# Interference stage of a complex-valued tower: inverse magnitudes moved from VectorE's reciprocal to ScalarE with a Newton step, four of the twelve weights begun on ScalarE, VectorE products joined

## The chip, the cores and the metric

The kernel is one program on one core of a Trainium2 chip. The metric is its device time in microseconds, the median of several executions. 0.2% (7 us) is about what a measurement can tell from no change.

## The reference, cut to what matters

A tower of 1024 tokens is encoded, passed through an attention, and then through the interference step below, with N = 4 complex vectors of D = 512 per token. R and I are the real and imaginary parts, `strength` is a 4x4 table per token (gathered embeddings).

```python
R = einsum('bnd,ned->bne', attn_r, int_Wr) - einsum('bnd,ned->bne', attn_i, int_Wi)
I = einsum('bnd,ned->bne', attn_r, int_Wi) + einsum('bnd,ned->bne', attn_i, int_Wr)
phase = arctan2(Ii * Rj - Ri * Ij, Ri * Rj + Ii * Ij)      # for every pair i, j
f = cos(phase) * strength[..., None]
sup_r = einsum('bijd,bjd->bd', f, R);  sup_i = einsum('bijd,bjd->bd', f, I)
norm = sqrt(sum(sup_r ** 2 + sup_i ** 2, axis=-1, keepdims=True) + 1e-08)
sup_r = sup_r / norm;  sup_i = sup_i / norm
```

The cosine of the phase between vectors i and j is the dot product of their unit vectors, element by element. The weight of vector j is strength[j,j] plus the sum over i of cosine(i,j) times strength[i,j].

## The kernel before

Five stages run one after the other: constants, first layers (tiles named a_), second layers (b_), attention (t_), interference (i_), top (e_). Only `phase_interfere` computes anything differently after the change. Its 1024 tokens are 8 tiles of 128. TensorE, for each tile and each n of 0 to 3, makes the real and the imaginary part of vector n, 48 matmuls of 128x512 in all (each product in three terms, L50 to L52), into one PSUM bank per part, so one tile fills all eight banks. Before it starts on vector n of tile t + 1, it waits for `unit`, that is, until VectorE has read vector n of tile t. It also waits for `negated`: ScalarE negates half of the loaded activations (`ng`, L1075), in a ring of two.

The tile then passes through three engines. `n` is the vector.

- ScalarE, `squares(t, n)`: square of the real part into `mag` (L1082) and of the imaginary part into `sqi` (L1085). The first may start only when the previous tile no longer needs `mag`.
- GpSimd, `add_squares`: their sum in `mag` (L1020).
- ScalarE, `magnitude(t, n)`: a mark for zero length (`zero`, Relu, L1089) and the root (`mag`, Sqrt, L1090).
- VectorE, `invert(n)`: reciprocal into `inv` (L1167). `unit_vector(n)`: both PSUM banks times `inv` into `cs` (L1175).
- The cosines of the pairs. Three of the six (`HELPED`: 0-1, 0-2, 1-2) are made by GpSimd, two products (L1037) and a sum (L1039) each; the other three by VectorE (L1188 to L1190). VectorE adds the mark `zz` (L1181, L1185 or L1191), and adds the cosine times its strength to two weights, which share the buffer of `inv`: L1199 where the weight is begun, L1196 afterwards.
- VectorE: weights times `mag` (L1223), then `cs` times weights for each part (L1225, two instructions of 2048 elements).
- GpSimd, `fold`: two sums over the four vectors (L1026, L1030). ScalarE and VectorE then scale `sup` by the inverse of its length (L1094 to L1100, L1152), a tile later.

GpSimd's order is fixed in its body: sums of squares 0 and 1, fold 0 of the last tile, sum of squares 2, fold 1, cosine 0-1, sum of squares 3, cosine 0-2, cosine 1-2. VectorE runs strictly in its program's order, and a `link` makes it wait for its own last instruction. Tiles 2 to 7 are turns of a hardware loop on VectorE and GpSimd. The top stage starts when the last `sup` is stored.

Of the kernel before, what the change touches and what calls it, by code (L numbers as in the profile page):

```python
# [9 lines left out]
ACT = mybir.ActivationFunctionType  # L10
# [4 lines left out]
P = 128  # L15
# [39 lines left out]
class Stage:  # L55


    def __init__(self, nc, tag):
        self.nc, self.tag, self.ctx = nc, tag, ExitStack()
# [4 lines left out]
    def sem(self, name):  # L64
        return self.ctx.enter_context(self.nc.semaphore(f"{self.tag}_{name}"))
# [5 lines left out]
def phase_constants(nc, g):  # L71
    s = Stage(nc, "c")
    with s.ctx:
        zeroed = s.sem("zeroed")
        made = s.sem("made")
        cols_in = s.sem("cols_in")
        block = s.ctx.enter_context(nc.Block())
# [29 lines left out]
def phase_first_layers(nc, g):  # L107
    s = Stage(nc, "a")
    XRAW = 4
    with s.ctx:  # L110
# [7 lines left out]
        hst = s.sb("hst", [P, TT, W])  # L118
        x_loaded = [s.sem(f"x_loaded{i}") for i in range(XRAW)]
        x_hi = s.sem("x_hi")  # L120
        x_split = s.sem("x_split")
        w_loaded = [s.sem(f"w_loaded{i}") for i in range(RAW)]
# [6 lines left out]
        bias_in = s.sem("bias_in")  # L129
        stored = [s.sem(f"stored{i}") for i in range(TT)]  # L130
# [105 lines left out]
def phase_second_layers(nc, g):  # L236
# [4 lines left out]
    with s.ctx:  # L241
# [42 lines left out]
        def _(pool):  # L284
# [4 lines left out]

            load_h(0, 0)  # L290
# [636 lines left out]
def phase_interfere(nc, g):  # L927
# [7 lines left out]
    STEPS = N + 1 + 3 * 2 + 3 * 4 + 1  # L935
    with s.ctx:
# [10 lines left out]
        t1 = s.sb("t1", [P, W])  # L947
        t2 = s.sb("t2", [P, W])
# [23 lines left out]
        chain = s.sem("chain")  # L972
        weighed = s.sem("weighed")
# [43 lines left out]
        def _(pool):  # L1017
# [4 lines left out]
            def fold(t, i):  # L1022

                if i == 0:
                    pool.wait_ge(weighed, t * 2 + 2)
# [44 lines left out]
        def _(act):  # L1070
# [7 lines left out]
            def squares(t, n):  # L1078
                act.wait_ge(multiplied, t * 8 + (2 * n + 2))
                if not (isinstance(t, int) and t == 0):  # L1080
                    act.wait_ge(chain, t * STEPS)
                act.activation(mag[:, n, :], g.ps[:, n, :], ACT.Square).then_inc(squared, 1)  # L1082
                if not isinstance(t, int) or 4 * t + n >= 2:
                    act.wait_ge(summed, t * N + (n - 1))
                act.activation(sqi[:, n % 2, :], g.ps[:, N + n, :], ACT.Square).then_inc(squared, 1)  # L1085

            def magnitude(t, n):
                act.wait_ge(summed, t * N + (n + 1))
# [3 lines left out]
            def length(t):  # L1092
                act.wait_ge(folded, t * 2 + 2)
                act.activation(sqi[:, :, :], sup[:, :, :], ACT.Square, accum_out=nrm[:, 0:1]).then_inc(len_done, 1)  # L1094
# [15 lines left out]
            def body(t, first, last=False):  # L1110
                squares(t, 0)
                if first:
                    negate(t, 2)
                magnitude(t, 0)
                squares(t, 1)
                if first:
                    negate(t, 3)
                magnitude(t, 1)
                squares(t, 2)
                magnitude(t, 2)  # L1120
# [17 lines left out]
            length(TT - 1)  # L1138
# [3 lines left out]
        def _(dve):  # L1142
# [5 lines left out]
            w = inv  # L1148
# [5 lines left out]
            def body(t, first):  # L1154
# [8 lines left out]
                def invert(n):  # L1163
                    dve.wait_ge(mag_done, t * N + (n + 1))
                    if not first and n == 0:
                        dve.wait_ge(weighed, t * 2)
                    link(dve.reciprocal(inv[:, n, :], mag[:, n, :]))  # L1167

                def unit_vector(n):
                    if not first and n == 0:  # L1170
                        dve.wait_ge(folded, (t - 1) * 2 + 1)
                    if not first and n == 2:
                        dve.wait_ge(folded, (t - 1) * 2 + 2)
                    for part in range(2):
                        dve.tensor_tensor(cs[:, part, n, :], g.ps[:, part * N + n, :], inv[:, n, :], ALU.mult).then_inc(unit, 1)  # L1175

                seen = set()

                def pair(i, j):

                    mark = dve.tensor_tensor(zz[:, :], zero[:, i, :], zero[:, j, :], ALU.add)  # L1181
                    if (i, j) in HELPED:
                        link(mark)
                        dve.wait_ge(helped, t * 9 + 3 * (HELPED.index((i, j)) + 1))
                        dve.tensor_tensor(t1[:, :], pc[:, 0, :], zz[:, :], ALU.add).then_inc(taken, 1)  # L1185
                        dve.wait_ge(taken, t * 3 + (HELPED.index((i, j)) + 1))
                    else:
                        dve.tensor_tensor(t1[:, :], cs[:, 0, i, :], cs[:, 0, j, :], ALU.mult)  # L1188
                        link(dve.tensor_tensor(t2[:, :], cs[:, 1, i, :], cs[:, 1, j, :], ALU.mult))
                        link(dve.tensor_tensor(t1[:, :], t1[:, :], t2[:, :], ALU.add))  # L1190
                        link(dve.tensor_tensor(t1[:, :], t1[:, :], zz[:, :], ALU.add))  # L1191
                    for a, b in ((i, j), (j, i)):

                        e = st[:, a * N + b:a * N + b + 1]
                        if b in seen:
                            ins = dve.scalar_tensor_tensor(out=w[:, b, :], in0=t1[:, :], scalar=e, in1=w[:, b, :],  # L1196
                                                           op0=ALU.mult, op1=ALU.add)
                        else:
                            ins = dve.tensor_scalar(w[:, b, :], t1[:, :], e, st[:, b * N + b:b * N + b + 1],  # L1199
                                                    ALU.mult, ALU.add)  # L1200
                            seen.add(b)
                    link(ins)

                invert(0)
                invert(1)
                unit_vector(0)
                unit_vector(1)
                invert(2)
                unit_vector(2)
                link(dve.tensor_copy(st[:, :], emb[:, bass.ds(t, 1), :].rearrange("p o x -> p (o x)")))  # L1210
                dve.wait_ge(unit, t * 8 + 12)
                pair(0, 1)
                invert(3)
                unit_vector(3)
                dve.wait_ge(unit, t * 8 + 16)
                pair(0, 2)
                pair(0, 3)
                pair(1, 2)
                if not first:
                    inverse_length(t - 1)  # L1220
                pair(1, 3)
                pair(2, 3)
# [513 lines left out]
```

## Time and profile before

| | us |
|---|---|
| median of 3 runs | 3566.72 (3565.09 to 3569.43) |
| span of the profiled execution | 3548.6 |
| interference stage in it, from its first weight load to the store of the last `sup` | 2807.3 to 3296.8 |
| last final multiplication ends | 3286.9 |

The profiled span starts at the first instruction and ends at the last; the 18.1 us between it and the median lie around it. In a row, the number behind the engine is the line of the kernel, and what stands in square brackets is how long the engine was idle before the instruction and what ended that. A group's row gives the shortest, the median and the longest duration in ns.

### The profile page before, as it was taken

The numbers are of one execution on the slowest core, as the hardware profiler recorded it, in microseconds if no ns is written. First come the engines' busy times: TensorE is split into PE (matmuls) and PEld (weight loads), VectorE is DVE, ScalarE is ACT, GpSimd is POOL, SyncE is SP. The second block draws the span as 40 slices with busy tenths as digits, with TensorE's granted clock in tenths as the row PEclk, the third lists the DMA queues.
The fourth block names the chain that finished last, engine by engine and source line by source line (L and its number), as shares of the span: only waits on it lengthen the run. The fifth ranks groups of instructions, "written<-read, shape, count | busy, mean of one in ns | idle before, by whom it ended". The sixth has DMA issues, their size and how long they took to land. (4 is left out here: it accounts for less than half of the span.)

```text
span 3548.6 us, 45531 instructions
## 1 busy us (share of the span) xinstructions
PE 3115.3 (88%) x16160; PEld 2659.5 (75%) x16160; DVE 1652.0 (47%) x3027; ACT 1168.9 (33%) x1986; POOL 388.2 (11%) x345
## 2 busy tenths in 40 slices
PE   8999999996999899995889989898989598884586
PEld 6888888885888788874778878887878476763575
DVE  3222222226211341114665566556655579999322
ACT  3111111114211241114554555455555432332332
POOL 1000000001111110010000000000000244543100
PEclk9999999998999999997998989898989799997798
DMA  5222222214333333323212221122112553442210
GB/s 181 71 71 71 71 71 71 71 59 163 113 95 95 113 118 94 93 74 128 78 47 56 62 71 47 49 70 71 47 47 72 136 102 83 89 85 45 95 36 6
DMA packets 364201, 285.38 MB, mean 80 GB/s; under 512 B 280048, under 2 KB 280176, under 8 KB 364016
## 3 DMA queue, kind: packets, MB, share of 16 engines
q1 hardware_dynamic: 341488, 206.97, 21.6%
q0 software_dynamic: 22656, 77.67, 6.3%
q8 instruction: 33, 0.54, 0.1%
q14 instruction: 24, 0.20, 0.0%
HBM read 194.40 MB, written 90.18 MB: 80 GB/s over the span
## 5 line engine op out<-in xcount | busy, mean ns | idle before, releaser
L50 PE MATMUL banks<-a_whi,a_xhi 128*128 128x512 f32 x1152 | 449.9, 391 | 24.0 <-DVE a_wlo L175 17.6
L51 PE MATMUL banks<-a_wlo,a_xhi 128*128 128x512 f32 x1152 | 448.8, 390 | 0.0
L52 PE MATMUL banks<-a_whi,a_xlo 128*128 128x512 f32 x1152 | 448.8, 390 | 0.0
L50 PE MATMUL banks<-b_ghi,b_whi 128*128 128x512 f32 x1024 | 401.8, 392 | 9.9 <-DVE b_slo L383 8.6
L51 PE MATMUL banks<-b_glo,b_whi 128*128 128x512 f32 x1024 | 398.9, 390 | 0.0
L52 PE MATMUL banks<-b_ghi,b_wlo 128*128 128x512 f32 x1024 | 398.8, 389 | 0.0
L175 DVE TENSOR_TENSOR a_wlo<-a_wraw,a_whi 128x512 fp32r<-128x512 f32 x144 | 99.6, 692 | 577.2 <-ACT a_whi L161 577.2
L50 PE MATMUL banks<-t_sx,t_whi 128*128 128x256 f32 x1024 | 307.7, 300 | 36.8 <-DVE t_wlo L791 26.9
L161 ACT ACTIVATE a_whi<-a_wraw 128x512 fp32r<-128x512 f32 x144 | 90.9, 632 | 667.7 <-PE banks L52 628.9
L51 PE MATMUL banks<-t_sx,t_whi 128*128 128x256 f32 x1024 | 295.7, 289 | 0.0
L368 DVE TENSOR_TENSOR b_wlo<-b_wraw,b_whi 128x512 fp32r<-128x512 f32 x128 | 88.2, 690 | 444.8 <-ACT b_whi L320 444.6
L52 PE MATMUL banks<-t_sx,t_wlo 128*128 128x256 f32 x1024 | 294.5, 288 | 0.0
L708 DVE TENSOR_SCALAR t_ks<-banks,cols 64x256 f32<-64x256 f32 x512 | 247.4, 483 | 97.5 <-PE banks L52 86.4
L50 PEld LDWEIGHTS banks<-a_whi,a_xhi 128*128 128x128 f32 x1152 | 216.6, 188 | 72.0 <-issue 17.6
L52 PEld LDWEIGHTS banks<-a_whi,a_xlo 128*128 128x128 f32 x1152 | 216.6, 188 | 45.2
L51 PEld LDWEIGHTS banks<-a_wlo,a_xhi 128*128 128x128 f32 x1152 | 216.7, 188 | 44.8
L50 PEld LDWEIGHTS banks<-t_sx,t_whi 128*128 128x128 f32 x1024 | 203.5, 199 | 43.2 <-DVE t_wlo L791 27.5
L50 PEld LDWEIGHTS banks<-b_ghi,b_whi 128*128 128x128 f32 x1024 | 192.7, 188 | 54.9 <-DVE b_slo L383 13.1
L320 ACT ACTIVATE b_whi<-b_wraw 128x512 fp32r<-128x512 f32 x128 | 80.2, 628 | 458.2 <-PE banks L52 457.5
L50 PE MATMUL banks<-i_whi,i_ax 128*128 128x512 f32 x384 | 159.3, 415 | 72.6 <-ACT i_ng L1075 38.1
L52 PEld LDWEIGHTS banks<-b_ghi,b_wlo 128*128 128x128 f32 x1024 | 192.4, 188 | 40.1
L51 PEld LDWEIGHTS banks<-b_glo,b_whi 128*128 128x128 f32 x1024 | 192.7, 188 | 39.0
(192 smaller groups left out, 6208.8 us busy)
## 6 DMA issues: line engine op xcount, KB each, us to landing
a_wraw<-w_first SPq DMA_DIRECT2D x144, 256.0 KB, 2.6
b_wraw<-w_second SPq DMA_DIRECT2D x128, 256.0 KB, 2.7
t_sx<-s_scr SPq DMA_DIRECT2D x64, 512.0 KB, 5.5
a_scr<-t_at SPq DMA_DIRECT2D x256, 128.0 KB, 1.9
i_ax<-a_scr SPq DMA_DIRECT2D x64, 512.0 KB, 5.9
h_scr<-a_hst POOLq DMA_DIRECT2D x72, 256.0 KB, 2.7
b_hl<-h_scr POOLq DMA_DIRECT2D x16, 1024.0 KB, 6.0
s_scr<-b_shi POOLq DMA_DIRECT2D x32, 512.0 KB, 4.4
```

The costliest lines, as they stand in the source:

```text
L50: mm(out, ahi, bhi, start=first, stop=False)
L51: mm(out, ahi, blo, start=False, stop=False)
L52: return mm(out, alo, bhi, start=False, stop=last)
L161: act.activation(whi[:, k % SPL, :], wraw[:, k % RAW, :], ACT.Copy).then_inc(w_hi, 1)
L175: dve.tensor_tensor(wlo[:, k % SPL, :], wraw[:, k % RAW, :], whi[:, k % SPL, :].bitcast(F32), ALU.subtract).then_inc(w_split, 1)
L320: act.activation(whi[:, j % SPL, :, :].rearrange("p a n -> p (a n)"), wraw[:, j % RAW, :], ACT.Copy).then_inc(w_hi, 1)
L368: dve.tensor_tensor(wlo[:, j % SPL, :, :].rearrange("p a n -> p (a n)"), wraw[:, j % RAW, :], whi[:, j % SPL, :, :].bitcast(F32).rearrange ...
L708: ins = dve.tensor_scalar(ks[half(at_half), m % 2, h, part, :], b_qk[half(h), 1, e * C:(e + 1) * C], bcol(M_K + e, m, half(h)), float(sign ...
```

## The change

Per tile, in the interference stage:

- VectorE's four reciprocals of 512 go. For two vectors at a time (q is 0 or 1), ScalarE takes the root s = Abs_reciprocal_sqrt(mag) and squares it, so y = s*s is roughly 1/mag. VectorE then does a Newton step, `tt = mag*y` and `inv = (tt - 2)*y` (that is minus 1/mag; the sign is undone in `rescale`).
- Relu, Sqrt and the two new activations run on 1024 elements. They wait for the sums of both vectors.
- The unit vectors of two n are one multiplication of 2048 elements out of four PSUM banks, which are renumbered by `bank(n, part)`. TensorE waits for two vectors at once.
- VectorE's own cosines take one product of 1024 in place of two of 512. The order of pairs becomes 0-1, 0-3, 0-2, 1-3, 1-2, 2-3.
- The copy of the strengths and the four instructions that begin the weights move to ScalarE (`strengths`, `begin`). GpSimd's second and third cosine wait for these.
- The multiplication by `mag` becomes two `rescale` of 1024, the first of which releases `mag` for vectors 0 and 1 before pair 2-3. The final multiplication is one of 4096.
- `negate` stands elsewhere in ScalarE's order, the scaling of `sup` comes after the begun weights.
- Outside the stage, GpSimd clears 11 semaphores at the start of the second layers, and semaphores are allocated in another order.

```diff
+    def bank(n, part):
+        return 4 * (n // 2) + 2 * part + n % 2
@@ gpsimd
-                pool.wait_ge(unit, t * 8 + (2 * N + 2 * j + 2))
-                pool.wait_ge(taken, t * 3 + x)
+                pool.wait_ge(unit, t * 2 + (j // 2 + 1 + 2))
+                if x == 0: ...
+                elif x == 1:
+                    pool.wait_ge(w_begun, t * 4 + 2)
+                else:
+                    pool.wait_ge(w_begun, t * 4 + 4)
+                    pool.wait_ge(taken, t * 3 + 1)
@@ scalar
+            def magnitude(t, q):
+                n = slice(2 * q, 2 * q + 2)
+                act.wait_ge(summed, t * N + (2 * q + 2))
+                act.activation(zero[:, n, :], mag[:, n, :], ACT.Relu, scale=-1.0 / LEAST, bias=k01[:, 1:2])
+                act.activation(mag[:, n, :], mag[:, n, :], ACT.Sqrt, bias=k01[:, 0:1]).then_inc(mag_done, 1)
+                act.wait_ge(mag_done, t * 6 + (3 * q + 1))
+                act.activation(sqi[:, :, :], mag[:, n, :], ACT.Abs_reciprocal_sqrt).then_inc(mag_done, 1)
+                act.wait_ge(mag_done, t * 6 + (3 * q + 2))
+                act.activation(sqi[:, :, :], sqi[:, :, :], ACT.Square).then_inc(mag_done, 1)
...
             def body(t, first, last=False):
+                negate(t, 3)
                 squares(t, 0)
-                if first:
-                    negate(t, 2)
+                squares(t, 1)
                 magnitude(t, 0)
-                squares(t, 1)
-                magnitude(t, 1)
                 squares(t, 2)
-                magnitude(t, 2)
                 if not last:
                     negate(t + 1, 0)
                 squares(t, 3)
-                magnitude(t, 3)
+                magnitude(t, 1)
+                strengths(t)
+                begin(t, 0, 1, 0, pc[:, 0, :], True)
                 if not last:
                     negate(t + 1, 1)
                 if not first:
-                    length(t - 1)
-                    scale(t - 1)
+                    length(t - 1, t * STEPS + SEED_READ[1])
+                begin(t, 0, 3, 1, tt[:, 0, :])
+                begin(t, 0, 2, 2, pc[:, 0, :])
                 if not last:
                     negate(t + 1, 2)
-                    negate(t + 1, 3)
+                if not first:
+                    scale(t - 1)
@@ vector
+                def unit_vectors(q):
+                    n = slice(2 * q, 2 * q + 2)
+                    dve.wait_ge(mag_done, t * 6 + (3 * q + 3))
+                    link(dve.tensor_tensor(tt[:, :, :], mag[:, n, :], sqi[:, :, :], ALU.mult))
+                    if not first:
+                        dve.wait_ge(weighed, t)
+                    link(dve.scalar_tensor_tensor(out=inv[:, n, :], in0=tt[:, :, :], scalar=2.0, in1=sqi[:, :, :],
+                                                  op0=ALU.subtract, op1=ALU.mult))
+                    if not first:
+                        dve.wait_ge(folded, t * 2 - (1 - q))
+                    dve.tensor_tensor(cs[:, :, n, :], g.ps[:, 4 * q:4 * q + 4, :]..., inv[:, n, :]..., ALU.mult).then_inc(unit, 1)
...
+                unit_vectors(0)
+                cosine(0, 1)
+                unit_vectors(1)
+                p = cosine(0, 3)
+                dve.wait_ge(w_begun, t * 4 + 2)
+                weigh(p, 3, 0)
+                p = cosine(0, 2)
+                weigh(p, 2, 0, taken)
+                dve.wait_ge(w_begun, t * 4 + 3)
+                p = cosine(1, 3)
+                weigh(p, 1, 3)
+                weigh(p, 3, 1)
+                dve.wait_ge(w_begun, t * 4 + 4)
+                p = cosine(1, 2)
+                weigh(p, 1, 2, taken)
+                weigh(p, 2, 1, taken)
+                dve.wait_ge(taken, t * 3 + 3)
+                rescale(0)
                 if not first:
                     inverse_length(t - 1)
+                p = cosine(2, 3)
+                weigh(p, 2, 3)
+                weigh(p, 3, 2)
+                rescale(1)
+                dve.wait_ge(w_scaled, t * 2 + 2)
+                dve.tensor_tensor(cs[:, :, :, :], cs[:, :, :, :], inv[:, :, :]..., ALU.mult).then_inc(weighed, 1)
```

`squares(t, n)` now waits for `rescale` of its pair in the tile before, and its second square, into `sqi`, for the Newton step that reads `sqi` last.

## Rows read from the trace of the kernel before

**Rows 1.** Busy time in a stretch of the stage: columns as in the first line.
```profile
core 0: us, PE busy (x) PEld busy (x) DVE busy (x) ACT busy (x) POOL busy (x), PEclk, DMA share, GB/s
2900.00:3000.00 100.00, 88.47 (x376) 70.70 (x374) 97.33 (x90) 30.23 (x53) 50.94 (x30) 0.98 0.43 88
```

**Rows 2.** Timeline of GpSimd: the first sum of squares of two tiles.
```profile
2959.86 2.28 POOL L1020 TENSOR_TENSOR i_mag<-i_mag,i_sqi 128x512 f32<-128x512 f32 x1 [19.20 <-ACT i_sqi L1085]
...
3013.89 2.27 POOL L1020 TENSOR_TENSOR i_mag<-i_mag,i_sqi 128x512 f32<-128x512 f32 x1 [19.63 <-ACT i_sqi L1085]
```

**Rows 3.** Timeline of TensorE: the first matmul of a third vector (n = 2).
```profile
3003.74 0.77 PE L50 MATMUL banks<-i_whi,i_ax 128*128 128x512 f32 x1 [6.00 <-ACT i_ng L1075]
```

**Rows 4.** Groups on the weights' and inverses' tile: ns min/median/max, first and last start.
```profile
L1196 DVE SCALAR_TENSOR_TENSOR i_inv<-i_t,i_st,i_inv x64: 743/750/1780, 2883.9 to 3279.3; 128x512 f32<-128x512 f32 x64
L1167 DVE RECIPROCAL i_inv<-i_mag x32: 3342/3353/3355, 2854.8 to 3253.6; 128x512 f32<-128x512 f32 x32
L1199 DVE TENSOR_SCALAR i_inv<-i_t,i_st x32: 540/1518/1621, 2871.9 to 3266.9; 128x512 f32<-128x512 f32 x32
...
L1223 DVE TENSOR_TENSOR i_inv<-i_inv,i_mag x8: 2291/2292/2294, 2903.9 to 3280.1; 128x2048 f32<-128x2048 f32 x8
```

**Rows 5.** Groups on the unit vectors' tile.
```profile
L1175 DVE TENSOR_TENSOR i_cs<-banks,i_inv x64: 679/681/693, 2861.9 to 3257.6; 128x512 f32<-128x512 f32 x64
...
L1026 POOL TENSOR_TENSOR i_cs<-i_cs x8: 4492/4612/4623, 2913.3 to 3287.0; 128x2048 f32<-128x2048 f32 x8
L1030 POOL TENSOR_TENSOR i_sup<-i_cs x8: 2337/2416/2437, 2919.2 to 3291.5; 128x1024 f32<-128x1024 f32 x8
```

**Rows 6.** Group on the magnitudes' tile.
```profile
L1020 POOL TENSOR_TENSOR i_mag<-i_mag,i_sqi x32: 1267/1294/2282, 2850.6 to 3247.7; 128x512 f32<-128x512 f32 x32
```

**Rows 7.** ScalarE, groups of the stage: busy us, mean ns | idle before.
```profile
L1100 ACT ACTIVATE i_sup<-i_sup,i_nrm 128x1024 f32<-128x1024 f32 x8 | 9.2, 1148 | 121.6 <-DVE i_nrm L1152 121.6
L1094 ACT ACTIVATE i_sqi<-i_sup 128x1024 f32<-128x1024 f32 x8 | 8.4, 1046 | 21.7 <-POOL i_sup L1030 21.7
```

**Rows 8.** Timeline of VectorE and GpSimd around cosine 1-2 of the third tile.
```profile
2988.52 0.43 DVE L1181 TENSOR_TENSOR i_zz<-i_zero 128x512 bf16<-128x512 bf16 x1
2989.07 0.69 DVE L1185 TENSOR_TENSOR i_t<-i_pc,i_zz 128x512 f32<-128x512 f32 x1
2989.80 1.62 DVE L1199 TENSOR_SCALAR i_inv<-i_t,i_st 128x512 f32<-128x512 f32 x1
2989.84 2.73 POOL L1037 TENSOR_TENSOR i_pc<-i_cs 128x512 f32<-128x512 f32 x2 [5.00 <-DVE i_t L1185]
2991.34 1.78 DVE L1196 SCALAR_TENSOR_TENSOR i_inv<-i_t,i_st,i_inv 128x512 f32<-128x512 f32 x1
2992.64 1.62 POOL L1039 TENSOR_TENSOR i_pc<-i_pc 128x512 f32<-128x512 f32 x1
2993.15 1.40 DVE L1181 TENSOR_TENSOR i_zz<-i_zero 128x512 bf16<-128x512 bf16 x1
```

**Rows 9.** Timeline where a tile begins: what runs beside fold 0.
```profile
2964.32 6.83 DVE L1167 RECIPROCAL i_inv<-i_mag 128x512 f32<-128x512 f32 x2
...
2965.80 4.62 POOL L1026 TENSOR_TENSOR i_cs<-i_cs 128x2048 f32<-128x2048 f32 x1
```

**Rows 10.** ScalarE's table loads: the interference stage's one, and a group of the attention.
```profile
2852.66 1.28 ACT L1090 ACT_TABLE_LOAD   x1
...
L671 ACT ACT_TABLE_LOAD x64 | 82.1, 1283 | 1.1
```

**Rows 11.** Timelines: the first tile's last squares, its final and the last final multiplications.
```profile
2873.65 0.60 ACT L1082 ACTIVATE i_mag<-banks 128x512 f32<-128x512 f32 x1 [3.75 <-PE banks L52]
...
2906.26 5.57 DVE L1225 TENSOR_TENSOR i_cs<-i_cs,i_inv 128x2048 f32<-128x2048 f32 x2
...
3282.40 4.49 DVE L1225 TENSOR_TENSOR i_cs<-i_cs,i_inv 128x2048 f32<-128x2048 f32 x2
```

**Rows 12.** GpSimd: the shortest instruction of the stage.
```profile
L1054 POOL MEMSET i_k<- 128x1 f32 x1 | 0.1, 98 | 1206.7 <-POOLq L500 1206.7
```

More of the change, by code:

```diff
@@ L1080, in squares @@
                 if not (isinstance(t, int) and t == 0):
[L1081 to L1088, printed above, removed]
+                    act.wait_ge(w_scaled, t * 2 - (1 - n // 2))
@@ new lines, in squares @@
+                act.activation(mag[:, n, :], g.ps[:, bank(n, 0), :], ACT.Square).then_inc(squared, 1)
+                if n >= 2:
+                    act.wait_ge(chain, t * STEPS + SEED_READ[0])
+                elif not (isinstance(t, int) and t == 0):
+                    act.wait_ge(chain, t * STEPS - (STEPS - SEED_READ[1]))
+                act.activation(sqi[:, n % 2, :], g.ps[:, bank(n, 1), :], ACT.Square).then_inc(squared, 1)
+            def magnitude(t, q):
+                n = slice(2 * q, 2 * q + 2)
+                act.wait_ge(summed, t * N + (2 * q + 2))
@@ new lines, in strengths, with begin @@
+            def strengths(t):
+                if not (isinstance(t, int) and t == 0):
+                    act.wait_ge(w_scaled, t * 2)
+                act.activation(st[:, :], emb[:, bass.ds(t, 1), :].rearrange("p o x -> p (o x)"), ACT.Copy).then_inc(st_in, 1)
+            def begin(t, i, j, order, of, both=False):
+                act.wait_ge(st_in, t + 1)
+                act.wait_ge(p_made, t * 3 + (order + 1))
+                for a, b in ((i, j), (j, i)) if both else ((i, j),):
+                    ins = act.activation(inv[:, b, :], of, ACT.Identity, scale=st[:, a * N + b:a * N + b + 1],
+                                         bias=st[:, b * N + b:b * N + b + 1])
+                    ins.then_inc(w_begun, 1)
@@ L1161, in link @@
                     dve.wait_ge(chain, t * STEPS + done[0])
[L1163 to L1175, printed above, removed]
@@ L1177, in body @@
[L1177 to L1181 removed]
+                def unit_vectors(q):
[8 more added lines that the diff above has]
+                        dve.wait_ge(folded, t * 2 - (1 - q))
+                    dve.tensor_tensor(cs[:, :, n, :], g.ps[:, 4 * q:4 * q + 4, :].rearrange("p (a n) w -> p a n w", a=2),
+                                      inv[:, n, :].unsqueeze(1).to_broadcast([P, 2, 2, W]), ALU.mult).then_inc(unit, 1)
+                    dve.wait_ge(unit, t * 2 + (q + 1 + 2))
@@ new lines, in cosine, with weigh, rescale @@
+                    return p
+                def weigh(p, a, b, last=None):
+                    ins = dve.scalar_tensor_tensor(out=inv[:, b, :], in0=p, scalar=st[:, a * N + b:a * N + b + 1],
+                                                   in1=inv[:, b, :], op0=ALU.mult, op1=ALU.add)
+                    if last is None:
+                        link(ins)
+                    else:
+                        ins.then_inc(last, 1)
+                def rescale(q):
+                    n = slice(2 * q, 2 * q + 2)
+                    dve.scalar_tensor_tensor(out=inv[:, n, :], in0=inv[:, n, :], scalar=-1.0, in1=mag[:, n, :],
+                                             op0=ALU.mult, op1=ALU.mult).then_inc(w_scaled, 1)
@@ L1219, in body @@
+                weigh(p, 1, 2, taken)
+                weigh(p, 2, 1, taken)
+                dve.wait_ge(taken, t * 3 + 3)
+                rescale(0)
                 if not first:
                     inverse_length(t - 1)
-                pair(1, 3)
-                pair(2, 3)
-                link(dve.tensor_tensor(w[:, :, :], w[:, :, :], mag[:, :, :], ALU.mult))
-                for part in range(2):
-                    dve.tensor_tensor(cs[:, part, :, :], cs[:, part, :, :], w[:, :, :], ALU.mult).then_inc(weighed, 1)
+                p = cosine(2, 3)
```

92 lines of the change are left out of this document (43 added, 49 removed).

## Prediction

> **What bounds the kernel now.** I looked first at where the changed stage lies in the span, then at how busy each engine is in it, then at one tile in the timelines. In the stage VectorE is busy 97% of the time, TensorE 88%, GpSimd 51% and ScalarE 30% [rows 1]. A tile takes 54.0 us: GpSimd's first sum of squares starts at 2959.86 in one and at 3013.89 in the next [rows 2]. TensorE's share of that is 0.87 x 54.0, some 47 us, and where it pauses it waits for `ng` [rows 3], which ScalarE makes late because it stands behind the scaling of `sup`, which waits for VectorE. So TensorE has some 7 us of slack per tile, and VectorE in its program's order sets the period. The obvious cost is the reciprocal, four of 3.35 us per tile [rows 4].
>
> Less obvious is what shares VectorE's time. Its instructions have two durations: the update of a weight 0.75 us or 1.78, the beginning of one 0.54 or 1.5 to 1.6 [rows 4]. The timeline shows which [rows 8]. GpSimd starts two products at 2989.84; VectorE's L1199 ends 1.07 us late, L1196 1.03 late, and the mark (0.43 when alone) 0.97 late. GpSimd's sum in its turn takes 1.62 in place of 1.29, and its sums of squares reach 2.28 [rows 6]. They take turns, an instruction each: one runs, the other waits for it to end. That holds for VectorE's instructions that read two tiles of SBUF and for L1199. It does not hold for the reciprocal, of which two take 6.83 us beside GpSimd's fold [rows 9], nor for the multiplication out of PSUM, of which the longest of 64 is 0.693 [rows 5]. In the kernel before, these two kinds fill exactly the time in which GpSimd folds (4.61 and 2.42 us [rows 5]) and sums.
>
> **The change, part by part.** Prices first. Two inputs of 512 take 0.69 us and of 2048 take 2.29 [rows 4, 8], so 1.04 ns per element more: 1.23 for 1024, 4.43 for 4096. The Newton step and `rescale`, of L1196's kind, take 0.75 + 0.53 = 1.28. The joined multiplication out of PSUM takes 0.68 + 1.60 = 2.28 [rows 5]. A wait for the own last instruction adds 0.04 [rows 8]. ScalarE's 1024 elements take 1.15 with a pointer for scale or bias (Relu, Sqrt) and 1.05 without (root, square) [rows 7]; I take 0.09 off where the next one does not wait.
>
> On VectorE itself this saves: 13.4 of reciprocals for 4 x 1.28 or so (5.1), four begun weights (2.2 alone, some 5 as they ran), and about 1.5 in the joined instructions. That is some 12 us per tile of work, and it would be the gain if VectorE stayed busy. I do not think it does. So I lay out one tile of the loop in order, with 0 at the end of the final multiplication of the tile before.
>
> 1. Fold 0 starts at once on GpSimd, 4.6 us. VectorE is next at `tt = mag*sqi`, which reads two SBUF tiles, so it is held until 4.65. (The turn of VectorE's loop is hidden below this.) Before, two reciprocals ran here.
> 2. `tt` 1.27, Newton 1.32, both unit vectors 2.28: 9.5.
> 3. GpSimd's next in order is the sum of squares 2. ScalarE can only write its `sqi` after the Newton step has read it (7.2), plus 0.6 for the square: the sum runs from 7.9 to 9.1, fold 1 to 11.5. VectorE's mark for pair 0-1 waits behind fold 1: 2.0 us.
> 4. GpSimd makes cosine 0-1, three instructions, 11.8 to 15.65. VectorE has nothing else in its order. The sum of squares 3 stands right behind on GpSimd and holds VectorE's join until 16.9.
> 5. Now ScalarE can begin on vectors 2 and 3: Relu, Sqrt, root, square, 4.3 with their waits, plus the table loads. The trace shows 1.28 for a load [rows 10]. It does not show whether Sqrt and Abs_reciprocal_sqrt share a table. The bounds are none and one at each change. The nearest rows are those of the attention, whose group has a load in each of its 64 steps where two functions alternate, so I take one before Sqrt and one before the root, 2.6 us: square done at 23.8. VectorE is idle from 17.6.
> 6. Unit vectors of 2 and 3, 4.9: 28.7.
> 7. Pair 0-3: mark, product of 1024, two sums, one weight, 4.0. GpSimd's cosine 0-2 runs beside it, three turns of 1.25 less the 0.13 gap, 3.4: 36.1. Pair 0-2: 2.0. Pair 1-3 with two weights 4.8, and cosine 1-2 beside it 3.4. Pair 1-2: 2.8. That is 49.1.
> 8. `rescale(0)` 1.2 and the small reciprocal 0.1: 50.4. It releases `mag`, so the next tile's squares and their two sums fall on pair 2-3 and the second `rescale`: 4.8 + 1.3 + 2 x 1.12 = 8.3. Final multiplication 4.4: 63.0.
>
> So the period is 63.0 against 54.0. The next tile's first magnitudes are ready in time: squares at 51.5, sums by 56, four activations and a load 5.6, some 62, before the fold is over. TensorE is released for vectors 0 and 1 at 9.5 and does them in 23.5. For the third it waits for `negate`, which stands behind the last begun weight (38.2) and is done at 39.4; for the fourth again, since that `negate` stands behind the scaling of `sup` (51.5) and is done at 52.7. Its last matmul ends at 64, or 66 with the slow start after a pause (0.77 us for a matmul [rows 3]). ScalarE asks for it at 63 + 8, behind the other squares, so some 5 us of cover are left; a load that came later than that would lengthen the tile. GpSimd's added waits (`w_begun`) end before VectorE's own pair does. The strengths' copy and the four begun weights lie on ScalarE, in idle time.
>
> The trace does not show a fold of 4.6 us against an instruction of two inputs, only sums of 1.29. Its bounds are 4.6 of holding, or, if the two share, none; I take 4.6, since every pair of rows 8 waits to the end. Without it the Newton step is done at 2.6 and the sum of squares 2 follows fold 0 directly, so item 3 ends 3.2 earlier.
>
> The first tile: its last squares start at 2873.65 [rows 11]. Add 1.1 for them, 1.3 for the sum, 6.9 for item 5, 4.9 for item 6 and 34.3 for items 7 and 8: 2922.1, against 2906.26 + 5.57 = 2911.8 before, 10.3 later. Seven tiles follow, 7 x 63.0, the last without a next tile's sums (2.3): 438.7, end 3360.8, against 3282.40 + 4.49 = 3286.9 before: 73.9 later. The last length needs a table load, 1.3. The 11 clears on GpSimd stand before its first load of the second layers; each is at least nothing and at most like its shortest instruction, 0.10 [rows 12], so 0 to 1.1, and I take 0.5. Sum: +75.7. The profiled span would be 3548.6 + 75.7 = 3624, and the median, 18.1 above it as before, **3642 us**, 2.1% slower.
>
> Two rules of the Trainium skill bear on this. "SBUF — State Buffer", section Who interferes with whom, has VectorE with two SBUF inputs and a GpSimd instruction that reads SBUF exclude each other for the whole instruction. Rows 8 agree for 1.29 us (1.03 late); by the rule the fold holds `tt` for its whole 4.6, which no row here shows. "ScalarE: Activation LUTs", section What ACT_TABLE_LOAD costs, counts a load as 1.28 and a drain of 1.38. The trace has the 1.28, and Sqrt began 0.02 after it, with no drain, so I leave the drain out. By the page a tile would take some 65.6 us and the kernel 3663. Its section Table sets has one expensive function per set, which would make these loads certain.
>
> **The rivals.**
>
> - *No loads, or a fold that does not hold.* One table serves both functions: 2.6 less per tile in eight, and 1.3 at the end, +54, 3621. With the fold free as well, 3.2 x 7 less: 3599.
> - *The turns are not taken where instructions are joined, and it gets faster* (the other side). For it: the product out of PSUM and the reciprocal never wait. Against it: rows 8, where three different kinds of instruction with SBUF inputs wait. Without any turns GpSimd reaches the end of its sum 3 at 13.3 in place of 16.9 (fold 0 at 4.65, the sum 1.25, fold 1 2.4, the cosine 3.8, the sum 1.25), item 7 loses 6.8 and item 8 loses 2.2: 12.6 less, 50.4 per tile. The first tile then ends 1.3 later than before, seven tiles take 352.8 against 375.1, and 1.8 is for the last load and the clears: -19, 3547. With no loads either, 48.0 per tile and 3527. The sum moves by 94.9 for these 12.6, so it decides at 10.1 less per tile, a period of 52.9.
> - *The change does all that it says*: VectorE, GpSimd and ScalarE hide behind TensorE. Then seven tiles take 47 in place of 375.1 / 7 = 53.6, 46 less, 3521. Against it is the order of GpSimd's body: cosine 0-1 is behind two folds, and magnitudes 2 and 3 behind that.
> - *TensorE becomes the bound at its lower clock.* It would pause some 16 us per tile in place of some 6 [rows 3]. If it stayed at the slow spacing (0.43 for 0.23) a tile would take 48 x 4 x 0.43 = 82 us and the kernel some 3790. Against it: with one pause per tile the granted clock of the stretch is still 0.98, nearly the full 2.4 GHz [rows 1].
>
> **How the numbers follow.** Forecast (61 to 66 per tile, 3628 to 3668): 0.72. No loads or a weaker fold (3597 to 3628): 0.11. Slow TensorE: 0.04. The turns not taken, or all hidden: 0.10. Within 0.2%: 0.03. The range 3597 to 3668 takes the first two, 0.83. Its upper end allows 1.5 per tile for the turn of the loop, if it is not hidden (a tile outside the loop took 2964.3 - 2911.8 = 52.5 [rows 9, 11], one in it 54.0), one more load of 1.28 per tile on the path, and 4 in the rest. Slower is 0.72 + 0.11 + 0.04 = 0.87, same 0.03, faster 0.10.
>
> **What the profile after would show.** ScalarE with some 4 table loads per tile, in magnitude and in length. VectorE's `tt` for vectors 0 and 1 with a longest of 4 to 5 us where 1.2 is its own, and ends with fold 0. VectorE idle before the join of pair 0-1 (GpSimd's cosine) and before `tt` of vectors 2 and 3 (ScalarE's square), together 8 to 10 us per tile. VectorE below 85% busy, TensorE near 75%, with its pause now ended by the unit vectors. A tile of 60 to 66 us from final multiplication to final multiplication. I am wrong if `tt` runs at 1.2 beside the fold, if the loads are missing, or if VectorE is busy throughout.

## Result: 3642.9 us against 3566.0, 2.2% slower

The changed kernel takes 3642.94 us (median of 4 executions, 3603.05 to 3649.15), the kernel before 3566.01 (4 executions, 3565.09 to 3569.43) on the same chip. The ratio is 1.0219, 95% interval 1.0143 to 1.0296. The forecast was 3642. A second set of 6 executions gave 3643.66 and 1.0228 (1.0166 to 1.029). Two executions of the runs below, 3765.63 us of sum3_early and 4194.97 of begin_alone, had a much lower clock than the others of their kernel and are in no ratio.

### The profile page after: what moved, and what is told of

Read it like the earlier page. It is cut to its first block and busy times, and to the rows that moved or that the text cites. A ratio compares the mean times of both kernels' runs of the same rounds, so it can differ in the third digit from the quotient of the medians.

```text
span 3647.3 us, 45563 instructions
## 1 busy us (share of the span) xinstructions
PE 3133.1 (86%) x16160; PEld 2673.5 (73%) x16160; DVE 1599.1 (44%) x2915; ACT 1277.3 (35%) x2069; POOL 426.4 (12%) x345
## 5 line engine op out<-in xcount | busy, mean ns | idle before, releaser
L50 PE MATMUL banks<-t_sx,t_whi 128*128 128x256 f32 x1024 | 308.3, 301 | 36.9 <-DVE t_wlo L797 27.5
```

The costliest lines, as they stand in the source:

```text
L50: mm(out, ahi, bhi, start=first, stop=False)
```

## The profile after

First the stretch view, as in [rows 1]. I give it for one tile, from one fold 0 to the next. The first fence is the kernel before, the second the changed kernel.

```profile
2965.80:3019.82 54.02, 46.16 (x193) 36.81 (x192) 52.25 (x51) 16.32 (x28) 25.23 (x17) 0.94 0.41 86
```

```profile
3003.78:3068.09 64.31, 48.20 (x193) 38.21 (x193) 43.85 (x36) 30.55 (x39) 31.47 (x17) 0.89 0.35 74
```

VectorE (the third busy time) went from 52.25 us per tile to 43.85: the change took 8.4 us of work off it, as it says. The tile grew by 10.3 us all the same. VectorE is now busy 68% of it, TensorE 75%, and no engine is the bound by its work. What bounds is the order in which the engines hand over. The view of waits, of the changed kernel from 2900 to 3300, names the hand-overs (total us, times, longest us):

```profile
DVE i_tt L1207 <- ACT i_sqi L1118: 87.6, 12, 8.3
...
ACT i_zero L1113 <- POOL i_mag L1034: 78.5, 12, 7.0
...
PE banks L50 <- DVE i_cs L1214: 53.4, 6, 10.1
...
DVE i_pc L1228 <- POOL i_pc L1060: 22.7, 6, 3.8
```

VectorE waits for ScalarE's square (L1118) twice per tile, ScalarE waits for GpSimd's sums, and VectorE waits for GpSimd's cosine 0-1. Now one tile's beginning in the timeline of the changed kernel, the place that answers to [rows 2, 8, 9] (rows of the three engines by start):

```profile
2991.40 1.15 ACT L1142 ACTIVATE i_sup<-i_sup,i_nrm 128x1024 f32<-128x1024 f32 x1 [10.45 <-DVE i_nrm L1193]
2992.57 1.28 ACT L1096 ACT_TABLE_LOAD   x1
2993.86 1.15 ACT L1096 ACTIVATE i_ng<-i_ax 128x512 fp32r<-128x512 f32 x2
2994.92 0.58 ACT L1103 ACTIVATE i_mag<-banks 128x512 f32<-128x512 f32 x1
...
2996.01 1.22 DVE L1246 SCALAR_TENSOR_TENSOR i_inv<-i_inv,i_mag 128x1024 f32<-128x1024 f32 x1
2996.06 7.76 POOL L1034 TENSOR_TENSOR i_mag<-i_mag,i_sqi 128x512 f32<-128x512 f32 x2 [10.79 <-ACT i_sqi L1108]
2997.27 5.40 DVE L1274 TENSOR_TENSOR i_cs<-i_cs,i_inv 128x4096 f32<-128x4096 f32 x1
3003.78 4.55 POOL L1040 TENSOR_TENSOR i_cs<-i_cs 128x2048 f32<-128x2048 f32 x1
3003.85 1.15 ACT L1113 ACTIVATE i_zero<-i_mag,i_k 128x1024 bf16<-128x1024 f32 x1 [6.89 <-POOL i_mag L1034]
3005.01 1.28 ACT L1114 ACT_TABLE_LOAD   x1
3006.30 1.15 ACT L1114 ACTIVATE i_mag<-i_mag,i_k 128x1024 f32<-128x1024 f32 x1
3007.47 1.28 ACT L1116 ACT_TABLE_LOAD   x1
3008.76 1.06 ACT L1116 ACTIVATE i_sqi<-i_mag 128x1024 f32<-128x1024 f32 x1
3009.85 1.06 ACT L1118 ACTIVATE i_sqi<-i_sqi 128x1024 f32<-128x1024 f32 x1
3010.94 1.23 DVE L1207 TENSOR_TENSOR i_tt<-i_mag,i_sqi 128x1024 f32<-128x1024 f32 x1 [8.27 <-ACT i_sqi L1118]
...
3021.79 1.76 DVE L1228 TENSOR_TENSOR i_pc<-i_pc,i_zz 128x512 f32<-128x512 f32 x1 [3.78 <-POOL i_pc L1060]
...
3030.14 1.22 DVE L1207 TENSOR_TENSOR i_tt<-i_mag,i_sqi 128x1024 f32<-128x1024 f32 x1 [6.58 <-ACT i_sqi L1118]
```

Read it from the GpSimd row at 2996.06. Two sums of squares, 1.27 us each when nothing stands in their way, take 7.76: the first runs when `rescale(1)` (L1246) is done, the second only when the final multiplication of 4096 elements (L1274) is done at 3002.67. That multiplication itself takes 5.40 in place of 4.43, since the first sum goes before it. Relu for the next tile starts at 3003.85, beside fold 0, with two table loads behind it, and VectorE's `tt` is 8.27 us late. ScalarE reached these squares late because it does the scaling of `sup`, a table load and a negation first (2991.40 to 2994.9). At 3021.79 VectorE waits 3.78 for cosine 0-1, at 3030.14 6.58 for the square of vectors 2 and 3. The three waits together are 18.6 us per tile.

Two groups give the turn-taking in durations (ns min/median/max), and four the table loads (us busy, mean ns), from 2870 to 3395:

```profile
L1207 DVE TENSOR_TENSOR i_tt<-i_mag,i_sqi x16: 1218/1226/5495, 2888.0 to 3348.5; 128x1024 f32<-128x1024 f32 x16
L1034 POOL TENSOR_TENSOR i_mag<-i_mag,i_sqi x32: 1262/1292/5476, 2878.2 to 3340.2; 128x512 f32<-128x512 f32 x32
```

```profile
L1116 ACT ACT_TABLE_LOAD x16 | 20.5, 1283 | 0.3
L1114 ACT ACT_TABLE_LOAD x15 | 19.2, 1283 | 0.1
L1138 ACT ACT_TABLE_LOAD x7 | 9.0, 1283 | 0.1
L1096 ACT ACT_TABLE_LOAD x6 | 7.7, 1283 | 7.8 <-DMA i_ax<-a_scr 7.7
```

There are 44 loads, six in a tile of the loop. Last, the ends of the first and last final multiplication, which answer to [rows 11]:

```profile
2938.44 4.43 DVE L1274 TENSOR_TENSOR i_cs<-i_cs,i_inv 128x4096 f32<-128x4096 f32 x1
...
3379.89 4.43 DVE L1274 TENSOR_TENSOR i_cs<-i_cs,i_inv 128x4096 f32<-128x4096 f32 x1
```

3384.3 - 2942.9 = 441.4 for seven tiles; it was 375.1.

## The experiments

My theory: the longer chain (squares, sums, Relu, two loads, root, square, Newton step) lies on the tile's path, and whole-instruction turns between VectorE and GpSimd stretch it. The rivals were that something outside the stage's arithmetic costs the time, that the table loads cost all of it, or that the joined instructions or the begun weights do.

Every kernel was timed against the kernel before on its own chip. Executions of one kernel spread over as much as 50 us (last section), so I also give the period of a loop tile, fold 0 to fold 0, and the length of the stage from its profile, from the first load of the strengths' ids to the first load of the top stage. Before, these are 54.0 and 511.4; changed, 64.3 and 589.7, in a pair of profiles on one chip.

| | ratio (95%) | tile | stage |
|---|---|---|---|
| changed, again | 1.0228 (1.0166 to 1.029) | 64.3 | 589.7 |
| frame_only | 0.9983 (0.9956 to 1.001) | 54.0 | 511.1 |
| no_table_loads | 1.0103 (1.0053 to 1.0153) | 58.3 | 551.1 |
| sum3_early | 1.0131 (1.0083 to 1.0178) | 58.9 | 547.6 |
| reciprocal_back | 1.012 (1.0075 to 1.0164) | 58.6 | 556.3 |
| final_in_two | 1.019 (1.0107 to 1.0272) | 62.2 | 579.9 |
| three_repairs | 1.0036 (0.9993 to 1.0078) | 55.5 | 528.2 |
| begin_alone | 0.9917 (0.9875 to 0.9959) | 50.0 | 484.3 |
| joined_alone | 1.0049 (1.0008 to 1.009) | 55.6 to 55.9 | 523.2 |
| two_helped_begin | 0.9876 (0.9816 to 0.9937) | 48.4 | 474.0 |

The tiles came out where they were expected, but for reciprocal_back (58.6 for 60 to 62) and two_helped_begin (48.4, just under 48.5 to 51). Four medians fell below their expected ranges: reciprocal_back 3597.08 (3613 to 3628), begin_alone 3529.92 (3533 to 3550), two_helped_begin 3512.37 (3520 to 3540) and three_repairs 3567.85 (3570 to 3590).

**The changed program around the old stage.** The clears and the order of semaphores as after, `phase_interfere` as before.

> The stage of before inside the changed frame: the 11 clears on GpSimd and the new order of semaphores alone. Forecast's term: +0 to +1.1 us, same as before within 0.2%. Rival: the frame moves the start of the interference stage (it began 2.4 us later in the changed kernel, and TensorE then stood for 18.6 us between its first two vectors with nothing recorded); then this kernel is 2 to 20 us slower than before. If the 18.6 us pause is an accident of an execution and not of the change, it turns up in some profiles of either kernel.

Tile 54.0, stage 511.1, 3562.55 us: no difference. The clears cost nothing that shows, and the time is lost in the stage.

**No table loads.** The root becomes a function that is loaded already.

```diff
-act.activation(sqi[:, :, :], mag[:, n, :], ACT.Abs_reciprocal_sqrt)
+act.activation(sqi[:, :, :], mag[:, n, :], ACT.Sqrt)
```

> The changed kernel with Sqrt in the place of Abs_reciprocal_sqrt (the inverse magnitudes are then wrong numbers), so that ScalarE needs one table only; six loads of 1.28 us per tile go. Theory of the path (a tile is a line of hand-overs, and two loads lie on it in magnitude 1, and where the second sum of squares is held by the final multiplication two or three more): 58 to 62 us per tile in place of 64.3, 15 to 45 us less than the changed kernel, 3600 to 3628. Rival (the tile is as long as VectorE's own work with its turns, ScalarE is 35% busy and its loads are hidden): 64.3 per tile, no difference to the changed kernel.

The tile fell from 64.3 to 58.3: 6.0 us for six loads of 1.28 (7.7), so most of this time lies on the path, and still 4.3 of the 10.3 remain without any. Here the next tile's sums get in before the final multiplication, and the fold then does what item 1 of the forecast said. The timeline of this kernel:

```profile
3054.63 1.22 DVE L1207 TENSOR_TENSOR i_tt<-i_mag,i_sqi 128x1024 f32<-128x1024 f32 x1
...
3054.79 5.41 POOL L1040 TENSOR_TENSOR i_cs<-i_cs 128x2048 f32<-128x2048 f32 x1 [5.63 <-DVE i_cs L1274]
...
3055.88 5.40 DVE L1210 SCALAR_TENSOR_TENSOR i_inv<-i_tt,i_sqi 128x1024 f32<-128x1024 f32 x1
```

The fold waits for `tt` (5.41 in place of 4.6), then `inv = (tt - 2)*y` waits for the whole fold and takes 5.40 in place of 1.22. That is the price which no row of before showed: a fold holds an instruction of two SBUF inputs for all its length. The Trainium skill, "SBUF — State Buffer", section Who interferes with whom, states it so, and these rows agree with it at 4.6 us.

**The sum of squares 3 ahead of fold 1** on GpSimd.

```diff
                 add_squares(t, 2)
+                add_squares(t, 3)
                 if not first:
                     fold(t - 1, 1)
                 cosine(t, 0)
-                add_squares(t, 3)
```

> The changed kernel with GpSimd's sum of squares 3 in front of fold 1 and cosine 0-1; the same instructions. Theory of the path: ScalarE starts magnitude 1 some 7 us earlier, of which the later pair 0-1 gives back 1 to 2; 57 to 60 us per tile, 30 to 50 us less than the changed kernel, 3593 to 3613. Rival (VectorE's work and turns set the tile): as many instructions and turns as before, less than 1 us per tile, 3636 to 3649.

58.9, as expected: 5.4 us for moving a 1.27 us instruction past a fold and a cosine. ScalarE no longer waits for fold 1 and cosine 0-1 before it can go on with vectors 2 and 3. The price is in one row, where VectorE now waits longer for cosine 0-1:

```profile
3099.13 0.69 DVE L1228 TENSOR_TENSOR i_pc<-i_pc,i_zz 128x512 f32<-128x512 f32 x1 [7.38 <-POOL i_pc L1060]
```

**Reciprocal back**, joined (1024 elements), in place of root, square and Newton step; all else as changed.

```diff
-                    link(dve.tensor_tensor(tt[:, :, :], mag[:, n, :], sqi[:, :, :], ALU.mult))
...
-                    link(dve.scalar_tensor_tensor(out=inv[:, n, :], in0=tt[:, :, :], scalar=2.0, in1=sqi[:, :, :],
-                                                  op0=ALU.subtract, op1=ALU.mult))
+                    link(dve.reciprocal(inv[:, n, :], mag[:, n, :]))
```

> The changed kernel with the Newton step undone: VectorE's reciprocal on 1024 elements (6.7 us) for each pair of vectors, no root of a reciprocal, no square, no table loads; everything else as changed. Theory of the path: the first reciprocal runs beside the fold, which held VectorE anyway, the second takes 6.7 where load, load, root and square (4.7) and the two Newton instructions (2.6) were: 60 to 62 us per tile, 15 to 30 us less than the changed kernel, 3613 to 3628, though VectorE works 8 us more per tile. Rival (the Newton step saves its 8 us, and other parts of the change cost): 72 us per tile, 3700.

58.6, better than the 60 to 62 expected. The costliest instruction of the old profile comes back and the tile gets 5.7 us shorter. Two things could explain it: the table loads go with the root, and the reciprocal takes no turns. The timeline shows the second:

```profile
3077.89 4.53 POOL L1040 TENSOR_TENSOR i_cs<-i_cs 128x2048 f32<-128x2048 f32 x1 [5.62 <-DVE i_cs L1265]
...
3077.91 6.55 DVE L1202 RECIPROCAL i_inv<-i_mag 128x1024 f32<-128x1024 f32 x1
```

The reciprocal's 6.55 us cover the fold's 4.53 completely, neither is stretched. But no_table_loads keeps the Newton step, drops only the loads, and has 58.3. So the 5.7 us are what the loads cost. The choice between reciprocal and Newton step, without loads, is worth 0.2 us, although the Newton step takes 8.2 us less of VectorE per tile (four of 1.22 for two of 6.55). Where those go can be read from the two timelines, each counted from the end of the final multiplication:

- Unit vectors 0 and 1 are done at 9.1 in both. The 4.1 us that VectorE saves there are the 4.2 by which the fold holds it.
- Cosine 0-1 is joined 1.7 later with the Newton step (16.7 for 15.0), because the square of vector 2 must wait until that step has read `sqi`, and GpSimd stands still for it (1.79). In reciprocal_back it waits for GpSimd's earlier sum alone.
- For vectors 2 and 3 the root and the square on ScalarE add 2.2 before VectorE can start. Of the second 4.1 saved, 1.9 is left.

The row is of no_table_loads, where VectorE starts on vectors 2 and 3:

```profile
3075.33 1.23 DVE L1207 TENSOR_TENSOR i_tt<-i_mag,i_sqi 128x1024 f32<-128x1024 f32 x1 [3.90 <-ACT i_sqi L1118]
```

**The final multiplication in two of 2048.**

```diff
-                dve.tensor_tensor(cs[:, :, :, :], cs[:, :, :, :], inv..., ALU.mult).then_inc(weighed, 1)
+                dve.tensor_tensor(cs[:, 0, :, :], cs[:, 0, :, :], inv[:, :, :], ALU.mult)
+                dve.tensor_tensor(cs[:, 1, :, :], cs[:, 1, :, :], inv[:, :, :], ALU.mult).then_inc(weighed, 1)
```

> The changed kernel with the final multiplication as two instructions of 2048 again. Theory of the turns: GpSimd's second sum of squares, which waited up to 5.4 us for the joined one, slips in between; magnitude 0 and the next tile start some 2 us earlier, 61.5 to 63 us per tile in place of 64.3, 10 to 20 us less. Rival (the two instructions only cost 0.1 more): no difference in the tile.

62.2: 2.1 us per tile for one more instruction on VectorE. The sum of squares gets in between the halves and not behind both.

**All three repairs**, the Sqrt of no_table_loads among them.

> The changed kernel with all three repairs: Sqrt in the place of Abs_reciprocal_sqrt (the inverse magnitudes are wrong numbers), the final multiplication in two, GpSimd's sum of squares 3 in front of fold 1. Theory of the path: each repair shortens a different link, but behind ScalarE's magnitude 1 the pairs with their turns remain (34 us); 55 to 57.5 us per tile, still over the 54.0 of the kernel before, 3570 to 3590. Rival (ScalarE's hand-over was all that cost): with it shortened by loads and order the tile falls under 54.0.

55.5, 8.8 under the changed kernel and still 1.5 over before. The singles (6.0, 5.4, 2.1) add up to 13.5, and 8.8 is left of them: in part they shorten the same path. Even so repaired, the change does not win.

**The begun weights alone**: the kernel before, with the strengths' copy and four begun weights on ScalarE.

```diff
+act.activation(inv[:, b, :], of, ACT.Identity, scale=st[:, a * N + b:...], bias=st[:, b * N + b:...]).then_inc(w_begun, 1)
...
-                            ins = dve.tensor_scalar(w[:, b, :], t1[:, :], e, st[:, b * N + b:b * N + b + 1],
-                                                    ALU.mult, ALU.add)
```

> The kernel before (in the changed frame) with one part of the change: the strengths' copy and the four begun weights on ScalarE, pair 0-2 joined in place. Theory of the turns: VectorE loses four instructions that reach 1.5 us because they wait for GpSimd; 50 to 52 us per tile in place of 54.0, stage 16 to 30 us shorter than before, 3533 to 3550 beside 3563. Rival (the hand-over to ScalarE and back costs what the instructions cost, 0.54 each): no difference within 5 us.

50.0 per tile, stage 27 us shorter, 0.8% faster in all. This part of the change is good, by 4.0 us per tile. In the group of updates the long form is gone (compare the first of [rows 4], whose longest was 1780):

```profile
L1238 DVE SCALAR_TENSOR_TENSOR i_inv<-i_t,i_st,i_inv x56: 743/751/752, 2877.3 to 3238.6; 128x512 f32<-128x512 f32 x56
...
L1229 DVE TENSOR_TENSOR i_t<-i_cs x24: 683/686/1789, 2871.4 to 3235.2; 128x512 f32<-128x512 f32 x24
```

The turns are not gone, as the second row shows. Those of cosine 1-2 now fall on the two products and the sum of pair 0-3 (1.79, 1.78 and 1.66 in place of 0.69 each). What the tile gains is the work of five instructions that left VectorE.

**The joined instructions alone**: the kernel before, with the product of 1024 and the final multiplication of 4096.

```diff
-dve.tensor_tensor(t1, cs[:, 0, i, :], cs[:, 0, j, :], ALU.mult)
-link(dve.tensor_tensor(t2[:, :], cs[:, 1, i, :], cs[:, 1, j, :], ALU.mult))
+link(dve.tensor_tensor(tt[:, :, :], cs[:, :, i, :], cs[:, :, j, :], ALU.mult))
```

> The kernel before (in the changed frame) with one part of the change: VectorE's product of 1024 for its own pairs and one final multiplication of 4096. Theory of the turns: the joined final multiplication keeps GpSimd's sum of squares 0 waiting for up to 4.4 us where it waited 2.2, so ScalarE's magnitude and the first reciprocal come later; 54.5 to 56 us per tile, 4 to 14 us slower than before. Rival (fewer instructions save their fixed part, 0.1 each): 53.5 us per tile, 3 to 5 us faster.

55.6 to 55.9 per tile, 1.6 to 1.9 worse, stage 12 us longer. VectorE saves overheads, but GpSimd's sum now takes up to 4.41, where [rows 6] had at most 2.28, and the magnitudes behind it come late, so that the first reciprocal starts 2.54 late:

```profile
L1026 POOL TENSOR_TENSOR i_mag<-i_mag,i_sqi x32: 1261/1295/4414, 2835.5 to 3257.1; 128x512 f32<-128x512 f32 x32
```

```profile
3075.64 3.35 DVE L1173 RECIPROCAL i_inv<-i_mag 128x512 f32<-128x512 f32 x1 [2.54 <-ACT i_mag L1096]
```

**A version for use**: begin_alone, the product of 1024, the final multiplication left in two, and pair 1-2 made by VectorE.

```diff
-HELPED = [(0, 1), (0, 2), (1, 2)]
+HELPED = [(0, 1), (0, 2)]
```

> The kernel before with the begun weights on ScalarE, the joined product of 1024, and pair 1-2 made by VectorE in place of GpSimd (two helped pairs, not three). Theory of the turns: GpSimd's three instructions of 1.27 us for this pair only displaced VectorE's; 48.5 to 51 us per tile, near TensorE's 47, stage 25 to 45 us shorter than before, 3520 to 3540. Rival (VectorE's own work sets the tile, and it gains 2.7 us of it): slower than the run with the begun weights alone by 2 us per tile, 3550 to 3565.

3512.37 us against 3563.96: 1.2% faster, the fastest of all, faster than both kernels. Its tile in the stretch view:

```profile
3026.30:3074.70 48.40, 44.64 (x194) 35.72 (x193) 46.69 (x45) 19.36 (x33) 20.66 (x13) 1.00 0.48 97
```

VectorE's busy time is 46.69 with one cosine more, 1.5 under begin_alone's 48.15: a product or sum that GpSimd takes over costs VectorE a turn of 1.0 to 1.1 each time [rows 8], three in a cosine, and a cosine that VectorE makes itself costs it 1.9 more (the product 1.22 and the sum 0.69; the mark and its sum are VectorE's either way). The joined product and the pair that comes back were not tried apart.

**Both kernels again.**

> The changed kernel once more, with a profile. If its tile is bistable (64.3 us where the second sum of squares waits for the joined final multiplication, 59 to 61 where it gets in before), the loop's tiles show one of the two; the stage takes 575 to 592 us, the median lies 75 to 85 us over that of the kernel before.

> The kernel before once more, for a second profile. If the pause of 18 to 21 us between TensorE's first and second vector is an accident that either kernel mostly has, it is here too, and the stage takes 511 us as in the run with the changed frame alone; if it belongs to the changed frame, the stage takes 495 us as in the first profile.

Tile 64.3 and 54.0, stage 589.7 and 511.4: +78.3, of which the first tile has 10.3 (from the start of the stage to its fold 0, 125.1 and 135.4), the seven others 67.9 (373.5 and 441.4), and the end nothing (12.8 and 12.9). The five tiles between the second and the last take 64.2 to 64.3 in both profiles, so the tile is not bistable. The medians differ by 96.9 and not by the 75 to 85 expected: on this chip ten of 17 executions of the kernel before took 3527 to 3548, which is the spread of the last section and not the stage.

## Why the prediction held, and where its steps did not

- **Direction and kind: right.** It said that the work saved on VectorE would not shorten the tile, because the chain of hand-overs grows. VectorE lost 8.4 us of work per tile and idles 18.6 in three waits; no_table_loads and sum3_early shorten the chain at two different places, by 6.0 and 5.4 us; reciprocal_back gives VectorE 8.2 us more work and the tile is still 5.7 shorter.
- **The first tile: right**, +10.3 for 10.3. (To about 1 us: the pause of the last section lies in it and was 0.8 shorter in the changed kernel. Against frame_only's 124.6 it is +10.8.)
- **Turns for a whole instruction: right**, and the rival without turns is out: joined instructions are held and hold (5.40 of the final multiplication, 5.48 of a sum), and final_in_two and joined_alone move the tile by about what the longest hold of a sum changed (5.48 to 3.34, and 2.28 to 4.41).
- **The other rivals are out.** The loads are there. TensorE did not become the bound: its stretch was granted 0.89 of the full clock, and it is busy 75% of a tile of 64.3, where the rival had 82 us of matmuls.
- **The end of item 8: mis-sized.** "The next tile's first magnitudes are ready in time: squares at 51.5, sums by 56" failed. The forecast itself had the scaling of `sup` end at 51.5 and the negation at 52.7, and then put the squares ahead of that negation, and it missed the table load in front of it. Really the squares start 7.7 us before the final multiplication ends, the second sum is held behind that multiplication, and Relu starts 1.2 after it. So the unit vectors 0 and 1 are done at 13.5 (forecast 9.5), the join is at 20.9 (16.9), `tt` of vectors 2 and 3 at 27.5 (23.8). In loop tiles it is ScalarE's square and not the fold that holds `tt`: `tt` takes 1.23 there, and the fold has ended. So the sign that I named, `tt` ending with fold 0, did not show. The fold holds VectorE only in the second tile (`inv`, 5.40) and in the last (`tt`, 5.50), and in the kernels where the sums got in.
- **The second half: shorter than forecast**, 36.8 for 39.2, from `tt` at 27.5 to the end at 64.3. The two sums do not take their turns in pair 2-3 (2.2 less), but one takes it in the final multiplication (1.0 more). The rest, 1.2, is in the estimates of single waits. Error and counter-error make 64.3 for 63.0. A second pair lies in the seven tiles: five tiles are 1.3 longer each than forecast, but the second tile took 60.8 and the last 59.3 (forecast 63.0 and 60.7), which leaves 441.4 for 438.7. That 3642.9 lies within 1 us of the 3642 is luck, and the changed executions alone spread from 3603 to 3649.
- **Loads: more than forecast**, six per loop tile for four: two at each magnitude, one at the length, and one in front of the negation at the loop's top. The forecast put 2.6 us of loads on the path, and its rival without loads took no more than that off a tile; no_table_loads prices them at 6.0. By the Trainium skill, "ScalarE: Activation LUTs", section What ACT_TABLE_LOAD costs, each would have a drain of 1.38 besides; here Sqrt starts 0.01 after its load (3005.01 + 1.28, 3006.30), so the drain does not show. (With two such drains on its path the forecast's estimate by the page should have been 65.8 per tile and some 3666, not 65.6 and 3663.) The last length needed no load (1.3 forecast, 0 measured).
- **VectorE's idle time: twice the forecast**, 18.6 for 8 to 10. The two waits that it named measured 10.4 (3.78 and 6.58); the third, 8.3, is the wait above, which it did not have. The busy shares (68% and 75%) are where they were put.
- **The 18.1 us between span and median were misread.** They do not lie around the span: after, the profiled execution took 3649.01 with a span of 3647.3, 1.7 more, and the repeat of before 3564.67 with 3562.9. What the first profile of before lacked is a pause of TensorE (last section): its stage took 495.3, that of the repeat 511.4. That the executions behind the median had this pause is inferred, since they left no trace. The sum of span terms (+75.7) stood for +78.3 of stage, so adding the 18.1 was right in number and wrong in reason.
- **0.2% was too fine.** Single executions differ by more than 1%, and the intervals of the ratios are 0.5 to 1.7% wide.

What each part is worth per tile: the begun weights -4.0, the joined instructions +1.6 to 1.9, root, square and Newton step for the reciprocal +5.7 (64.3 against 58.6), which is the table loads (6.0) and nothing besides. If they add up, which no run shows, they give 57.4 from 54.0; the remaining 6.9 are with what reciprocal_back shares with the changed kernel, work by two vectors and the new order of ScalarE and GpSimd. sum3_early shows that one place in this order holds 5.4 of such time. Grouping and order were not separated, so how the 6.9 divide between them is not shown.

## What to carry to other kernels

Before replacing a slow instruction, look at what it covers and at what the new ones need. Here the new instructions were 8.2 us per tile shorter on VectorE, but the fold, the wait for `sqi` and the extra work on ScalarE left 0.2 of that, and the functions that alternate on ScalarE cost 6.0 in table loads. Where two engines take turns by the instruction, joining instructions lengthens what the other must wait for; join where nothing urgent is queued on the other side, and keep a gap where something is. And when work is moved between engines that hand over several times per tile, write out the whole order of each queue for one tile, table loads and negations included: the place where the forecast left out a load and a negation was the one that was wrong.

## What the runs showed of the hardware that I had not expected

- **A pause of TensorE with nothing recorded.** Between its first and its second vector of the stage TensorE stands still for 18.6 to 21.0 us in twelve of thirteen profiles, among them a repeated one of the kernel before; in the first profile of before it did not (0.47). The two rows are of the changed kernel and of that repeat:

```profile
2855.66 0.79 PE L50 MATMUL banks<-i_whi,i_ax 128*128 128x512 f32 x1 [18.62 <-issue]
```

```profile
2853.94 0.77 PE L50 MATMUL banks<-i_whi,i_ax 128*128 128x512 f32 x1 [20.85 <-issue]
```

In the repeat ScalarE's first square, which waits for the first vector's matmuls and not for the second's, starts only as TensorE goes on:

```profile
2853.57 0.60 ACT L1082 ACTIVATE i_mag<-banks 128x512 f32<-128x512 f32 x1 [10.13 <-remote]
```

So it seems to be the end of the first vector that comes late, and not another engine that keeps TensorE waiting. Why is open. It is not of the change, since frame_only and the repeat have it.
- **A granted clock that differs between executions.** In the attention stage, which none of the kernels changes, it was 0.91 in one profile and 0.96 in another, and the interference stage began 37.8 us sooner in the latter (2766.7 for 2804.5). The rows are of before and of reciprocal_back. This is why periods and stage times tell these kernels apart better than medians.

```profile
1700.00:2700.00 1000.00, 898.98 (x5812) 813.55 (x5812) 605.21 (x1510) 543.89 (x1005) 0.00 (x0) 0.91 0.22 59
```

```profile
1700.00:2700.00 1000.00, 892.68 (x6025) 813.14 (x6024) 626.71 (x1564) 563.72 (x1040) 0.00 (x0) 0.96 0.22 59
```

- **The clock granted in a tile differs between the kernels**: 0.94 before, where TensorE is busy 85% of the tile, 0.89 changed (75%), 1.00 in two_helped_begin (92%). The 193 matmuls of the changed tile take 48.20 us, the 194 of the fastest one 44.64.
